# Five small reorderings and a wider column sum in an attention-plus-experts layer on one core

## The reference

```python
x = x + attn(layernorm(x))        # x: 4 x 1024 x 256, 16 heads of 64
x = x + ffn(layernorm(x))         # 8 experts, inner width 512, two per token

# attn: Nystrom attention with 64 landmarks per head (means over 16 tokens)
attn1 = softmax(q @ k_l.T); attn2 = softmax(q_l @ k_l.T); attn3 = softmax(q_l @ k.T)
# pinv: z = attn2.T / (max(column sums) * max(row sums)), then six steps of
#       z = 0.25 * z @ (13 I - az @ (15 I - az @ (7 I - az))),  az = attn2 @ z
out = attn1 @ pinv(attn2) @ (attn3 @ v)
out = out + conv13(out) ; out = out @ w_fc + b_fc

# ffn: logits = x @ router.T; top two experts, each with a softmax over the logits
#      within 2% of it; out += weight * (silu(x @ gate.T) * (x @ up.T)) @ down.T
```

## Time and profile before

| | |
|---|---|
| median of 3 runs | 1077.02 us (1073.0 to 1077.06) |
| profiled execution | 1074.41 us |
| its span, first to last instruction | 1072.4 us |
| granted TensorE clock, mean | 0.992 |
| TensorE busy | 1032.1 us (96%) |

### The profile page before, as it was taken

How to read it: one execution, slowest core, us unless ns; L and a number is a source line. 1 busy time by engine, 2 the same in 40 slices (tenths; PEclk the granted TensorE clock), 3 DMA queues, 4 the chain that set the end, 5 groups by cost and what they waited for, 6 DMA issues and landing times.

```text
span 1072.4 us, 20581 instructions
## 1 busy us (share of the span) xinstructions
PE 1032.1 (96%) x7924; PEld 824.9 (77%) x7924; DVE 637.0 (59%) x1364; ACT 304.5 (28%) x501; POOL 378.4 (35%) x344
## 2 busy tenths in 40 slices
PE   4999899999999999999999999989999999999996
PEld 4788788888888856667766667768787877878795
DVE  7257757677648776768777777755424334243332
ACT  4333223232235522323331332321212122121210
POOL 5003122221235513153554455552233333433333
PEclk9999999999999999999999999999999999999998
DMA  9462000000300130312432232533432223322112
GB/s 331 185 11 3 1 1 1 1 1 1 105 4 3 42 157 21 108 59 73 146 109 66 73 110 89 188 87 74 89 50 50 43 43 53 50 51 39 25 21 30
DMA packets 89992, 69.58 MB, mean 65 GB/s; under 512 B 47600, under 2 KB 82960, under 8 KB 88880
## 3 DMA queue, kind: packets, MB, share of 16 engines
q1 hardware_dynamic: 76032, 48.31, 16.4%
q0 software_dynamic: 13440, 16.93, 9.0%
q10 hardware_dynamic: 432, 3.15, 0.7%
HBM read 42.74 MB, written 26.66 MB: 65 GB/s over the span
## 4 chain that ended last, share of the span: by engine, by line
PE 85%; DVE 5%; DMA 3%; issue 3%; POOL 2%; ACT 1%; POOLq 0%; another core or an unknown queue 0%; SPq 0%; DVEq 0%; ACTq 0%
PE ps L1904 17%; PE ps L1818 9%; PE ps L1795 9%; PE ps L1562 9%; PE ps L1550 9%; PE ps L1947 9%; PE ps L1810 5%; PE ps L1888 2%; PE ps L1622 2%; PE ps L1629 2%; DMA out<-mem 1%; PE ps L1867 1%; PE ps L1506 1%; PE ps L1941 1%; POOL xs_d L643 1%
## 5 line engine op out<-in xcount | busy, mean ns | idle before, releaser
L1904 PE MATMUL ps<-mem 128*128 128x256 f32 (+1 forms) x1120 | 221.3, 350 | 0.0
L1904 PEld LDWEIGHTS ps<-mem 128*128 128x128 f32 x1120 | 188.9, 190 | 28.1 <-issue 7.5
L670 POOL DMA_INDIRECT out<-mem x60 | 102.1, 1702 | 184.8 <-DVE mem L1363 138.2
L1351 DVE TENSOR_TENSOR mem<-mem,ps 128x512 f32<-128x512 f32 x66 | 45.4, 688 | 156.3 <-PE ps L1904 135.0
L1818 PE MATMUL ps<-mem 128*128 128x264 f32 x512 | 122.3, 392 | 0.1
L891 ACT ACTIVATE mem<-ps 128x512 f32<-128x512 f32 x66 | 39.4, 597 | 283.3 <-PE ps L1904 238.0
L1947 PE MATMUL ps<-mem 128*128 x480 | 115.1, 383 | 3.6 <-DVE mem L1351 2.2
L1550 PE MATMUL ps<-mem 128*128 128x256 f32 x512 | 115.4, 384 | 0.0
L1562 PE MATMUL ps<-mem 128*128 128x256 f32 x512 | 115.2, 382 | 0.0
L1795 PE MATMUL ps<-mem 128*128 128x512 f32 x256 | 115.1, 593 | 0.0
L629 POOL TENSOR_TENSOR mem<-mem,small 128x1024 f32<-128x1024 f32 x32 | 60.9, 1904 | 140.9 <-DVE small L1278 140.7
(11 more groups left out here) (226 smaller groups left out, 1298.0 us busy)
## 6 DMA issues: line engine op xcount, KB each, us to landing
mem<-w_gu SPq DMA_DIRECT2D x9, 1024.0 KB
mem<-xs_d SPq DMA_DIRECT2D x22, 260.0 KB, 2.9
mem<-x SPq DMA_DIRECT2D x8, 512.0 KB, 7.3
mem<-x SPq DMA_DIRECT2D x32, 128.0 KB, 2.2
out<-mem SPq DMA_DIRECT2D x32, 128.0 KB, 1.7
mem<-w_down SPq DMA_DIRECT2D x8, 512.0 KB
xnt_d<-mem ACTq DMA_DIRECT2D x3, 1024.0 KB, 7.8
mem<-xnt_d SPq DMA_DIRECT2D x3, 1024.0 KB, 4.8
```

The lines of the kernel that those rows point to most:

```text
L670: pool.indirect_dma_start(out=out_rows, out_offset=bass.IndirectOffsetOnAxis(ap=rows_to.bitcast(U32), axis=0), in_=ys[:, r % YRING], in_of ...
L1351: dve.tensor_tensor(hid[:, n % 2], sil[:, n % 2], bank(2 + n % 2), ALU.mult).then_inc(s("m_hid"), 1)
L1904: mm = pe.matmul(bank(2 * c + n % 2)[:, i * size:(i + 1) * size], w[:, k, c, f * P:(f + 1) * P], xst[:, a % 2, k, 0:size], start=(k == 0), ...
```

## The change

- GpSimd raises `a_rs` ahead of the two operations that make `nb`; ScalarE waits for a new `a_nb`, and `nb` is left out for b=3.
- `router_columns` comes ahead of the statistics of batch 1, and `sums_down(E)` ahead of all transposes.
- `c1_inverse_sums(1)` and `c1_tokens_out(1)` move from m=2 to m=1, the second behind `c1_first_max(3)` and ahead of `c1_max(3)`.
- `column_sums` becomes 8 products of 512 columns, with 32 columns of ones as weights, into banks 4 and 5; DVE takes the maximum over 1024 columns.
- The exponential of the gaps waits for the two gaps (`d_gap`) and not for the whole choice.
- `add_bias` of one tile moves behind scatters of group 5; the ones behind it each move by one step.
- ScalarE does two of the last group's `norm_rows` after `gate_out(1)`, the gap exponential and `rows_transposed(1)`.
- TensorE does `c2_y(MT - 1)` ahead of `x_columns(0)`.

```diff
                     ch.link(pool.tensor_tensor(r, r, w, ALU.mult))
-                ch.link(pool.tensor_tensor(w, mv[:, b, :, 0], r, ALU.mult))
-                pool.tensor_scalar(nb[:, b], w, -1.0, 0.0, ALU.mult, ALU.add).then_inc(s("a_rs"), 1)
+                pool.sem_inc(s("a_rs"), 1)
+                if ACT_ROWS[b]:
+                    ch.link(pool.tensor_tensor(w, mv[:, b, :, 0], r, ALU.mult))
+                    pool.tensor_scalar(nb[:, b], w, -1.0, 0.0, ALU.mult, ALU.add).then_inc(s("a_nb"), 1)
...
                     weigh(QT - 1)
                     add_bias(LAST_SUMS - 1)
-                    add_bias(LAST_SUMS)
-                if i >= QT and y_tile(i) is not None and y_tile(i) + 2 < MT:
-                    add_bias(y_tile(i) + 2)
+                if i >= QT and y_tile(i) is not None and y_tile(i) + 1 < MT:
+                    add_bias(y_tile(i) + 1)
...
             def normalise(b):
-                act.wait_ge(s("a_rs"), b + 1)
+                if ACT_ROWS[b]:
+                    act.wait_ge(s("a_nb"), b + 1)
...
-                act.wait_ge(s("d_hot"), g + 1)
+                act.wait_ge(s("d_gap"), 2 * g + 2)
...
-            for v in range(G):
-                norm_rows(NG - 1, v)
+            norm_rows(NG - 1, 0)
+            norm_rows(NG - 1, 1)
             gate_out(1)
             gap_exponentials(NG - 1)
             rows_transposed(1)
+            norm_rows(NG - 1, 2)
+            norm_rows(NG - 1, 3)
             gate_out(2)
...
             row_statistics(0)
+            router_columns()
             for b in range(1, B):
                 row_statistics(b)
-                if b == 1:
-                    router_columns()
...
                 if m + 1 < NP2:
                     c1_less_max(m + 1)
-                if m >= 2:
+                if m == 1:
+                    c1_inverse_sums(1)
+                if m >= 3:
                     c1_inverse_sums(m - 1)
                     c1_tokens_out(m - 1)
...
                 if m + 2 < NP2:
                     c1_first_max(m + 2)
+                if m == 1:
+                    c1_tokens_out(1)
                 if m == 4:
                     dve.wait_ge(s("b_cols"), 1)
-                    dve.tensor_reduce(zz[:, 1:2], bank(7)[:, 0:NQ], AX, ALU.max).then_inc(s("b_sums"), 1)
+                    dve.tensor_reduce(zz[:, 1:2], bank(4, 2), AX, ALU.max).then_inc(s("b_sums"), 1)
...
-                    ch.link(dve.tensor_tensor(gap[:, c, 0:n], bc(top[:, c, 0:n]), lg, ALU.subtract))
+                    dve.tensor_tensor(gap[:, c, 0:n], bc(top[:, c, 0:n]), lg, ALU.subtract).then_inc(s("d_gap"), 1)
+                    dve.wait_ge(s("d_gap"), 2 * g + c + 1)
...
+            pe.wait_ge(s("r_made"), 1)
+            sums_down(E, brw).then_inc(s("r_mm"), 1)
...
-                        if c == 2:
-                            pe.wait_ge(s("r_made"), 1)
-                            sums_down(E, brw).then_inc(s("r_mm"), 1)
...
-                for q in range(NQ):
-                    for r in halves:
-                        mm = pe.matmul(bank(7)[r, q:q + 1], zt[r, q], ones[r, 0:1], start=True, stop=True)
+                for g in range(4):
+                    for h, r in enumerate(halves):
+                        mm = pe.matmul(bank(4 + h)[32 * g:32 * g + 32], ones[r, 0:32], zt[r, 8 * g:8 * g + 8].rearrange("p q c -> p (q c)"),
+                                       start=True, stop=True)
...
             c2_counts(NG - 2)
-            x_columns(0)
             pe.wait_ge(s("c2_x1"), MT - 2)
             c2_y(MT - 1)
+            x_columns(0)
```

## The result

The changed kernel takes 1061.91 us (median of 4 runs, 1061.12 to 1063.27), the kernel before 1076.02 beside it on the same chip (1073.0 to 1077.06). The forecast was 1063.5 us, with a range of 1059.5 to 1069.5. The profiled execution took 1063.27 us, the longest of the four, and has a span of 1061.4.

A forecast was written before the change was run, and what follows sets the result against it. TensorE, busy for 96% of the span, was taken as the bound. Terms 0.45+5.4+2.7+1.8+2.0 = 12.35 us gave 1062.1 from 1074.41 us and 1064.7 from the median 1077.02; forecast 1063.5, range 1059.5 to 1069.5.

The forecast's parts named there:

- The beginning: First transposes: signalling a_rs earlier lets DVE start b=3 sooner and removes TensorE's wait, 0.45 us (0 to 0.5).
- Softmax scaling: At sim2(2): the 5.19 us wait goes, the pair runs at high clock, c1_v3(1) starts 5.4 us earlier (3.6 to 5.6).
- The margin ahead of c1_v3(2): c1_tokens_out(2) was to finish before c1_v3(2) needs it, with the margin shrinking from 1.4 to some 0.2 us.
- Column sums: Eight wide products take 1.1 us, saving 2.7 (2.0 to 2.9), plus 1.8 for the clock behind them (0 to 1.8).
- Experts' first blocks: From c2_y(31) to down(1): 0.7 us at hidden(0) plus 1.3 from down(1)'s wait, 2.0 us in all (0.7 to 2.1).
- a wait that no engine explains: Ahead of ScalarE's gate_out(1), which came at 697.24; gate_out(1) was to come earlier, removing down(1)'s wait, 1.3 us.
- the forecast's own sign: The prediction is wrong if x_columns(3) does not come 2 us sooner relative to c2_y(30).
- The 0.7 us at hidden(0, 0): With c2_y(31) ahead of the transposes, hidden(0) starts at about 687.7 in place of 688.4.
- The sum: All terms, 0.45+5.4+2.7+1.8+2.0 = 12.35 us, giving 1062.1 from 1074.41 us or 1064.7 from the median 1077.02.
- some four: Microseconds of TensorE waits listed near 684, 698 and 721 when the prediction read the profile.
- the end gives only 0.7: Rival: ScalarE's unexplained wait turns up elsewhere and delays the gap exponential or hidden_out(1); 1065 us, chance 0.10.
- the others: Other rivals: clock or margin 1065.5 to 1067.5, 0.15; wide products serial 1069.5, 0.05; within 0.5% 1072, 0.05; slower, 0.03.

The follow-up runs named there:

- e3: Kernel before with only the part on the experts' first blocks; 1072.57 us, ratio 0.999 to the kernel before.
- e4: Kernel before with only the part on the beginning; 1076.51 us in one run.
- e1: Kernel before with only the softmax part (c1_inverse_sums(1) and c1_tokens_out(1) moved to m=1); 1067.55 us, ratio 0.9946.
- e5: The changed kernel run again for a second profile; 1061.26 us, ratio 0.9881 to the kernel before.
- e6: The changed kernel without its part on the experts' first blocks; 1061.52 us, ratio 0.9882 to the kernel before.
- e9: The changed kernel with all four groups of wide column sums in the same 32 output partitions; 1063.83 us in one timed execution.
- e12: The changed kernel with x_columns(0) in the middle of c2_y(31), run a second time; 1062.35 us, ratio 0.9871 to the kernel before.
- e8: The changed kernel with column sums as 64 products again, each with 32 moving columns of ones; 1065.89 us in one timed execution.
- e10: The changed kernel with x_columns(0) inside c2_y(31), plus 24 filler products of constants ahead of x_columns(3); 1063.99 us, ratio 0.988 to the kernel before.
- e11: The changed kernel with x_columns(0) inside c2_y(31), plus 12 filler products of constants ahead of x_columns(3); 1060.75 us, ratio 0.9858 to the kernel before.

## Why the forecast was right in its time, and where a step failed

- *The beginning, 0.45 us.* Right in the mechanism: the wait ahead of batch 3's transposes is gone. L1513 comes 0.42 us sooner in the profile after and 0.4 to 0.6 in the others, which is no more than the old beginning differs from itself.
- *Softmax scaling, 5.4.* Right in each step: no wait ahead of sim2(2), the pair at 2.08, DVE's less_max(3) at 110.14 (110.5 forecast), c1_v3(1) at 115.13 (115.6) with a new wait of 1.27 (1.3), the clock at 1.00 through it. 5.42 in the whole change, 5.43 alone. The margin ahead of c1_v3(2) held. The 5.4 is the price of one execution; in e3 and e4 the old order costs 1.1 to 1.2 us more.
- *Column sums, 2.7 and 1.8 for the clock.* Right: 2.8 and 1.7 between the two profiles; the clock's share is larger, up to 3.2, in other executions of the old sums, so the upper bound of 1.8 was too low. The reason given for the clock, that wide products keep more of the array busy, was not worked out from any row; the run with 32 columns shows, in one profile, that moving more than one column was enough.
- *Experts' first blocks, 2.0.* Wrong: 0.2 between the two profiles (18.27 and 18.09 from counts(6) to counts(7)), and no difference in the medians. The step that failed is "With two norm_rows behind it, gate_out(1) comes before DVE is done with choices(7)". The forecast counted on the new order of ScalarE to move "a wait that no engine explains" out of the way. gate_out(1) waited for TensorE's signal, which rose 3.61 us behind the end of the products before and 3.97 after, whatever ScalarE did; ScalarE stood idle for 5.38 us. Where the signals are in time there is no wait at down(1) to remove. By the forecast's own sign this part was wrong: x_columns(3) comes 0.44 us sooner relative to c2_counts(6), right behind c2_y(30), and not 2 (38.65 us for 39.09). The 0.7 us at hidden(0, 0) came out as 0.6 in this pair of profiles, and as 0 to 0.2 or, beside e1, as a loss of 0.6 against the other profiles of the old order.
- *The sum.* The parts give 1.8 us less than forecast, and about half of that was made up by what is not of the change. From first_square to the start of c2's stage the same code took 89.7 to 90.8 us in different profiles, 90.80 in before and 90.02 in after; and from there to counts(6) 296.18 in before and 295.78 in after. That is 1.2 us of the 11.5 by which TensorE ended sooner. So the trace reads 0.42 + 5.42 + 4.50 + 0.18 for the parts, 0.78 + 0.40 of spread, less 0.21 between counts(7) and block 4: 11.49. The end of the span takes back 0.5, so the profile pair gained 11.0 us, and the forecast had added up 12.35.
- *The time.* That 1061.91 us came out so near 1063.5 is in part luck. The medians fell by 14.1 us, more than the profile pair, since before has a spread of 4 us and its median lies above its profiled execution, while after was profiled in its slowest. Measured again on another chip (e5) the median fell by 12.4 us, and by 12.15 without the blocks part (e6).
- *A slip without effect.* The waits near 684, 698 and 721 are 1.41, 1.22 and 2.34 us, 5.0 in all and not "some four". Nothing was worked out from it.

The rival "the end gives only 0.7" came nearest on its part, for the reason that it names; the others did not happen.

What stays open is what makes the signals late. They were late in before, after and e9 to e12, and in time in e1 to e8; kernels measured together share a chip (e1 to e4, e5 to e8, e9 and e10, e11 and e12) and were alike in this. In all six profiles with late signals the last of this stretch rose 1.7 to 1.8 us behind the end of GpSimd's last indirect DMA of group 6, as 685.77 behind 683.08 + 0.96 in after. The same DMAs did no harm in e5. That they coincide in time is all I have; no run takes those DMAs away.

## What to carry to other kernels

A wait that the profile puts down to no engine should be priced at zero gain until something shows who ends it; take a second profile of the same kernel before building on a wait of a us or two. When TensorE's work moves up ahead of a wait for a transfer, look at that wait before counting the gain: here 0.9 us won ahead of one went to a longer wait (0.3) and a slower clock behind it (0.6). What fills the wait itself promises more, but price it from a row of the same form, since fillers that overran it by 3.4 us lost more than they won. The products with one moving column cost twice here, in their weight loads and in the clock of what followed.

## What the runs showed of the hardware that was not expected

- With 64 products of one moving column the clock fell to 0.50 against their end or behind them in four of four profiles, although TensorE counted as busy all through; the same number of products with 32 columns took the same 3.9 us and left it at 1.00 (one profile).
- Where the clock falls depends on the execution: behind the same narrow sums it was low from 151.3 to 154.7 in the profile of before and from 150.3 to 157.1 in e3, and at an idle wait of 3.09 us in e9 it did not fall at all, while it did at one of 2.34 us in before. At down(1) it fell behind 2.10 us in e10 and not behind 2.14 in e12.
- Four column tiles of 32 times two row halves ran 512-column products 6.6 times as fast as one after another would be (1.09 us, and 7.2 estimated from c1_sim's rate); the row halves give 2.0 of that (3.62) and the column tiles 3.3.
- Some of TensorE's semaphores rose up to 4.0 us behind the recorded end of their product in before, after and e9 to e12 (3.97 in after, 3.60 in e11), and none more than 0.25 us in e1 to e8.
